# Row maxima of two attentions as pairs of 16-bit numbers, turned by 16-bit products, and their subtraction put first in each run on the row halves

## What is computed

```python
q = (layer_norm(x) @ wq)   # 20 heads of 64
k = (ctx @ wk); v = (ctx @ wv)   # ctx is layer_norm(x) itself in the self-attention
scores = einsum('bhnd,bhmd->bhnm', q, k) * 64 ** -0.5
attn = softmax(scores, axis=-1)
out = einsum('bhnm,bhmd->bhnd', attn, v)
x = out @ wo + bo + x
```

## Time and profile before

| | |
|---|---|
| Time, median of 3 runs | 1470.73 us |
| The profiled execution: its time, its span | 1475.56 us, 1473.8 us |
| TensorE matmuls (PE) busy | 1360.7 us, 92% |
| TensorE weight loads (PEld) busy | 1169.2 us, 79% |
| VectorE (DVE) busy | 1025.4 us, 70% |
| ScalarE (ACT), GpSimd (POOL) busy | 748.2 us, 751.0 us (51% each) |
| Mean granted clock of TensorE | 0.929 of full speed |
| Self-attention: maxima from, last weighing | 353.9 us, about 737 us |
| Cross-attention: maxima from, last weighing | 766.5 us, about 1372 us |

### The profile page before, as it was taken

One profiled execution on the slowest core, in us unless ns is written; L12 is line 12 of the kernel. 1 busy time (PEld: TensorE's weight loads), 2 busy tenths in 40 slices (PEclk: granted clock), 3 DMA queues, 4 the chain that ended last, 5 costly groups with the idle time before them and its releaser, 6 DMA issues. The chain is left out here.

```text
span 1473.8 us, 38650 instructions
## 1 busy us (share of the span) xinstructions
PE 1360.7 (92%) x16460; PEld 1169.2 (79%) x16460; DVE 1025.4 (70%) x1902; ACT 748.2 (51%) x1356; POOL 751.0 (51%) x510
## 2 busy tenths in 40 slices
PE   4989899885999999999979999999999999999597
PEld 3777777764888898889857888888888888888587
DVE  4577777746777867786657777777777767665485
ACT  2356565552555554555425545454555555554264
POOL 2266777565434443444514545454555555455364
PEclk9588888967999999999978999999999999999699
DMA  5001110002000000000010000000010000000000
GB/s 131 12 10 46 47 32 2 2 2 65 2 2 2 2 2 2 2 2 2 2 39 7 2 7 2 7 2 7 2 45 2 2 2 2 2 2 2 12 15 23
DMA packets 31955, 20.33 MB, mean 14 GB/s; under 512 B 21414, under 2 KB 30314, under 8 KB 31786
## 3 DMA queue, kind: packets, MB, share of 16 engines
q1 hardware_dynamic: 31786, 17.86, 4.7%
HBM read 16.54 MB, written 1.31 MB: 12 GB/s over the span
## 5 line engine op out<-in xcount | busy, mean ns | idle before, releaser
L507 POOL TENSOR_TENSOR cross_probs_l<-cross_probs 128x1024 f16<-128x1024 f32 x160 | 303.6, 1897 | 276.5 <-ACT cross_probs L578 276.2
L578 ACT ACTIVATE cross_probs<-cross_score 128x1024 f32<-128x1024 f32 x160 | 163.9, 1024 | 249.9 <-PE cross_score L820 249.9
L507 POOL TENSOR_TENSOR self_probs_l<-self_probs 128x1024 f16<-128x1024 f32 x80 | 151.5, 1894 | 204.0 <-ACT self_probs L578 203.6
L675 DVE TENSOR_REDUCE cross_maxima<-cross_max 128x2 f32<-128x1024 f32 x160 | 194.6, 1216 | 7.4 <-PE cross_max L796 7.2
L1591 POOL TENSOR_TENSOR ad_probs_l<-ad_probs 128x1024 f16<-128x1024 f32 x64 | 120.8, 1893 | 97.7 <-ACT ad_probs L1668 97.0
L578 ACT ACTIVATE self_probs<-self_score 128x1024 f32<-128x1024 f32 x80 | 82.1, 1027 | 156.8 <-PE self_score L820 156.8
L840 PEld LDWEIGHTS cross_pv<-cross_v_h,cross_probs 128*128 128x128 bf16 x1280 | 116.6, 98 | 33.2 <-issue 28.2
L840 PE MATMUL cross_pv<-cross_v_h,cross_probs 128*128 128x65 bf16 x1280 | 135.3, 196 | 2.6 <-POOL cross_probs_l L507 2.6
L661 DVE TENSOR_TENSOR cross_qk_l<-cross_shared,cross_qk_h 128x256 fp32r<-128x256 f32 (+1 forms) x160 | 87.9, 556 | 69.0 <-ACT cross_qk_h L563 68.8
L841 PE MATMUL cross_pv<-cross_v_l,cross_probs 128*128 128x64 f16 x1280 | 133.9, 194 | 0.0
L842 PE MATMUL cross_pv<-cross_v_h,cross_probs_l 128*128 128x65 bf16 x1280 | 133.5, 193 | 0.0
(11 more groups left out here) (420 smaller groups left out, 4735.5 us busy)
## 6 DMA issues: line engine op xcount, KB each, us to landing
ad_ctx_rows<-in_ctx SPq DMA_DIRECT2D x8, 192.0 KB, 2.8
cross_ctx_rows<-in_ctx SPq DMA_DIRECT2D x8, 192.0 KB, 2.5
sw_raw<-in_L_xattn_wq SPq DMA_DIRECT2D x2, 640.0 KB, 6.2
sw_raw<-in_L_xattn_wk SPq DMA_DIRECT2D x2, 640.0 KB, 4.3
sw_raw<-in_L_xattn_wv SPq DMA_DIRECT2D x2, 640.0 KB, 3.8
cw_raw<-in_L_xattn_wq SPq DMA_DIRECT2D x2, 640.0 KB, 4.1
lr_raw<-in_L_xattn_w_ff SPq DMA_DIRECT2D x2, 640.0 KB
out<-x_rows SPq DMA_DIRECT2D x8, 160.0 KB, 1.9
```

The lines of the kernel that those rows point to most:

```text
L507: nc.gpsimd.tensor_tensor(probs_l[:, n % PR, :, :].rearrange("p j k -> p (j k)"), whole, whole.bitcast(BF16)[:, 1::2], ALU.subtract).then_ ...
L578: nc.scalar.activation(probs[:, n % PR, :, :].rearrange("p j k -> p (j k)"), score_bank[:, :], ACT.Exp, scale=SCALE).then_inc(exped, 1)
L675: nc.vector.reduce_max(out, scores, AX.X).then_inc(max_read, 1)
```

## The change

Four things change in `attention`, in both attentions:

1. `reduce_max` writes float32 maxima to a small tile `top`. GpSimd writes them as a bfloat16 number and the bfloat16 remainder to columns 0 and 1 of `maxima`, which is now a bfloat16 tile (`split_maxima`, two instructions on 128x4 elements for each pair). It stands in GpSimd's list ahead of the low part of the last round of the slot.
2. "mt" waits for that (`max_split`) instead of `max_read`, and turns the two blocks by bfloat16 products with a bfloat16 identity, instead of float32 transposes.
3. `turned` and `minus` are bfloat16. The product with minus ones adds both parts.
4. The product with minus ones leaves `score` for a function `less_max`, and is issued ahead of `find_max`.

```diff
--- before.py
+++ after.py
@@ -392,7 +392,8 @@
         half_neg = sb("half_neg", [P, QT], F32)
         eps = sb("eps", [P, QT], F32)
         stats_seen = sb("stats_seen", [P, QT], F32)
-        minus = sb("minus", [P, P], F32R)
+        minus = sb("minus", [P, P], BF16)
+        ident_b = sb("ident_b", [P, P], BF16)
 
         xn = sb("xn", [P, QT, 2, P], F32)
         stats = sb("stats", [P, QT, 6], F32)
@@ -410,8 +411,9 @@
         qk_l = sb("qk_l", [P, KEPT, SEQ + KD], F32R)
         v_h = [sb(f"v_h{i}", [P, KT, HEADS, DV], BF16) for i in range(2)]
         v_l = [sb(f"v_l{i}", [P, KT, HEADS, DH], F16) for i in range(2)]
-        maxima = sb("maxima", [P, 2, QT, 2, DH], F32)
-        turned = sb("turned", [P, 2, SEQ], F32R)
+        top = sb("top", [P, 2, QT, 2], F32)
+        maxima = sb("maxima", [P, 2, QT, 2, DH], BF16)
+        turned = sb("turned", [P, 2, SEQ], BF16)
         PR = 2 * ROUNDS
         probs = sb("probs", [P, PR, 2, 512], F32)
         probs_l = sb("probs_l", [P, PR, 2, 512], F16)
@@ -446,6 +448,8 @@
         qk_hi = sem("qk_hi")
         max_filled = sem("max_filled")
         max_read = sem("max_read")
+        max_hi = sem("max_hi")
+        max_split = sem("max_split")
         scored = sem("scored")
         exped = sem("exped")
         probs_split = sem("probs_split")
@@ -491,17 +495,27 @@
                 pool.wait_ge(wo_hi, 1)
                 nc.gpsimd.tensor_tensor(wo_hl[:, :, 1, :], background.wo, wo_hl[:, :, 0, :], ALU.subtract).then_inc(wo_split, 1)
 
+            def split_maxima(batch, p):
+
+                b, _ = batch
+                pool.wait_ge(max_read, b * RB + (p + 1) * ROUNDS)
+                nc.gpsimd.tensor_copy(maxima[:, p % 2, :, :, 0], top[:, p % 2, :, :]).then_inc(max_hi, 1)
+                pool.wait_ge(max_hi, b * PAIRS + p + 1)
+                nc.gpsimd.tensor_tensor(maxima[:, p % 2, :, :, 1], top[:, p % 2, :, :], maxima[:, p % 2, :, :, 0],
+                                        ALU.subtract).then_inc(max_split, 1)
+
             def slot(kind, s, cur, prev, nxt):
                 if s == 2 and nxt is not None:
                     inverse_root(nxt[0])
                 if s == 4 and prev is not None:
                     rows = x[:, bass.ds(prev[0] * QT, QT), :]
                     nc.gpsimd.tensor_tensor(rows, rows, bo_row[:, None, :].to_broadcast([P, QT, HID]), ALU.add).then_inc(x_bo_ready, 1)
-                if (work := before(s, SCORE, cur, prev)) is not None:
-                    (b, _), p = work
-                    for r in range(ROUNDS):
+                for r in range(ROUNDS):
+                    if r == ROUNDS - 1 and (work := before(s, MAX, cur, prev)) is not None:
+                        split_maxima(*work)
+                    if (work := before(s, SCORE, cur, prev)) is not None:
+                        (b, _), p = work
                         n = p * ROUNDS + r
-
                         pool.wait_ge(exped, b * RB + n + 1)
                         whole = probs[:, n % PR, :, :].rearrange("p j k -> p (j k)")
                         nc.gpsimd.tensor_tensor(probs_l[:, n % PR, :, :].rearrange("p j k -> p (j k)"), whole,
@@ -517,7 +531,8 @@
             pool.wait_ge(filler, 1)
             inverse_root(0)
 
-            nc.gpsimd.memset(minus[:, :].bitcast(F32), -1.0)
+            nc.gpsimd.memset(minus[:, :], -1.0)
+            nc.gpsimd.tensor_copy(ident_b[:, :], ident[:, :])
             nc.gpsimd.memset(maxima[:, :, :, :, :], 0.0)
             for i in range(2):
                 ins = nc.gpsimd.memset(v_h[i][:, :, :, DH:DV], 1.0)
@@ -668,9 +683,9 @@
                         (b, _), p = work
                         dve.wait_ge(max_filled, b * RB + p * ROUNDS + r + 1)
                         if cross:
-                            out, scores = maxima[:, p % 2, r, :, 0], max_bank[:, :].rearrange("p (j k) -> p j k", j=2)
+                            out, scores = top[:, p % 2, r, :], max_bank[:, :].rearrange("p (j k) -> p j k", j=2)
                         else:
-                            out = maxima[:, p % 2, :, :, 0].rearrange("p t j -> p j t")
+                            out = top[:, p % 2, :, :].rearrange("p t j -> p j t")
                             scores = max_bank[:, :].rearrange("p (j t k) -> p j t k", j=2, t=QT)
                         nc.vector.reduce_max(out, scores, AX.X).then_inc(max_read, 1)
                     if s == 3 and r == 0 and nxt is not None:
@@ -802,17 +817,19 @@
                                                   qk_h[half, at, t * P:(t + 1) * P], qk_h[half, at, SEQ:SEQ + KD], start=True, stop=True)
                 mm.then_inc(max_filled, 1)
 
-            def score(r, work):
+            def less_max(r, work):
 
                 (b, parity), p = work
-                at = kept(parity, p)
-                n = p * ROUNDS + r
                 if r == 0:
                     pe.wait_ge(shifted, b * PAIRS + p + 1)
-                after(pe, exped, b * RB + n)
+                after(pe, exped, b * RB + p * ROUNDS + r)
                 for j, half in enumerate(HALF):
                     nc.tensor.matmul(score_bank[:, j * 512:(j + 1) * 512].rearrange("p (c q) -> p c q", c=2), minus[half, :],
                                      turned[half, p % 2, None, :].to_broadcast([DH, 2, SEQ]), start=True, stop=False)
+
+            def score(r, work):
+                (b, parity), p = work
+                at = kept(parity, p)
                 for c in range(2):
                     keys = slice(SEQ + (2 * r + c) * P, SEQ + (2 * r + c + 1) * P)
                     for m, (ks, qs) in enumerate(((qk_h, qk_h), (qk_h, qk_l), (qk_l, qk_h))):
@@ -846,6 +863,8 @@
             def slot(kind, s, cur, prev, nxt):
                 period = cur[0] if cur is not None else NB
                 for r in range(ROUNDS):
+                    if (work := before(s, SCORE, cur, prev)) is not None:
+                        less_max(r, work)
                     if (work := before(s, MAX, cur, prev)) is not None:
                         find_max(kind, s, r, work, period)
                     if (work := before(s, SCORE, cur, prev)) is not None:
@@ -856,10 +875,10 @@
                         if key[0] == "mt":
                             (b, _), p = before(s, MT, cur, prev)
                             bank_ = claim(kind, period, key)
-                            pe.wait_ge(max_read, b * RB + (p + 1) * ROUNDS)
+                            pe.wait_ge(max_split, b * PAIRS + p + 1)
                             for t in range(QT):
-                                mm = nc.tensor.transpose(bank_[:, t * P:(t + 1) * P],
-                                                         maxima[:, p % 2, t, :, :].rearrange("p j c -> p (j c)"), ident[:, :])
+                                mm = nc.tensor.matmul(bank_[:, t * P:(t + 1) * P], maxima[:, p % 2, t, :, :].rearrange("p j c -> p (j c)"),
+                                                      ident_b[:, :], start=True, stop=True)
                             mm.then_inc(filled, 1)
                         elif key[0] == "weigh":
                             weigh(kind, s, key[1], before(s, WEIGH, cur, prev))
```

10 lines of the change are left out of this document (5 added, 5 removed).

## The result

The changed kernel takes 1451.74 us (median of 4 runs, 1449.74 to 1455.42), the kernel before beside it 1469.87 us (4 runs, 1464.77 to 1471.73): ratio 0.987, interval 0.985 to 0.989. It is 18 us faster. I had forecast 42 us, a time of 1429. The time lies inside the range that I had stated, 1418 to 1456, but by luck: the range reached that high only for two rivals, neither of which holds as I had put it, and the sum's own range ended at 1437.

The account below looks back on a forecast made before the run. TensorE's instruction pace was taken to bound both attentions. 26.4 + 19.7 - 2 - 1.4 - 1 = 41.7 us saved, median 1470.7 to 1429 us; range 1418 to 1456, the sum's own 1420 to 1437.

Parts of the forecast that it names:

- opening of the runs: Start of each run on TensorE: 16-bit minus ones first save 0.11 us in 240 runs, 26.4 us.
- turned maxima: Turning on TensorE: 16-bit products save 0.11 us before F32R (108) and 0.15 otherwise (52), 19.7 us.
- GpSimd (tight pairs, once): Delayed low parts cost 2 us over 16 tight pairs; late split maxima in the first self-attention batch cost 1.4 us once.
- last slots: Waits moved to the front of the run cost 1 us, in the last slots, where little lies between runs.
- as slow as the 4-byte one: Bound on the opening: if a 16-bit load on a row half is that slow (187 ns), it saves nothing.
- the first rival: The opening gains nothing, by a slow half-row load or a pause between types: 16 us saved, 1455 us; chance 0.13.
- 0.12, 0.23, 0.23: Expected TensorE distances in us: last `weigh` product to minus ones, these to maxima, maxima to scores.
- The slower pace: Turned maxima at the skill's 81 ns per 128-column product: pair 0.16 instead of 0.11 us, term 8 us smaller.
- comes off the time nearly in full: Both attentions: TensorE sets the pace, so savings between two starts in its timeline shorten the time almost fully.
- one slot per batch where it leads: Against the no-change rival (1468 us, chance 0.05): VectorE, at 74%, leads in only one slot per batch.
- 0.4 us are left: Worst cross-attention slot: the delayed low part ends at about 1012.3, `weigh` needs it at 1012.78; two pairs in ten so tight.
- GpSimd's order costs more: Rival: a pair of small instructions takes 1.4 us, stalling 16 tight pairs, 11 us more, 1440 us; chance 0.09.

Follow-up runs that it names:

- one16_maxima_first: `one16` with the minus ones put back behind the maxima, leaving only the turned maxima by 16-bit products: 1461.00 us, ratio 0.994 to the kernel before.
- one16: The changed kernel without its GpSimd part; reduce_max writes each maximum once as a 16-bit number, no split: 1434.48 us.
- 1: Experiment 1, the run `one16`: the changed kernel without its GpSimd part, each maximum kept as one 16-bit number: 1434.48 us.
- 2: The changed kernel, but in the self-attention alone GpSimd issues the low part first and splits the maxima behind it: 1441.58 us.
- 3: The kernel before plus only GpSimd's wait for the maxima ahead of the last low part, no new work: 1478.94 us.
- 10: Experiment 10, the run `one16_norm_later`: `one16` with VectorE taking the second round's maxima before splitting the layer norm, cross-attention only: 1447.83 us.
- one16_norm_later: `one16`, but in the cross-attention VectorE takes the maxima of a slot's second round before splitting the layer norm: 1447.83 us.
- maxima_first: The changed kernel with the minus ones back behind the maxima, so the maxima open the run again: 1471.04 us.

## Why the prediction was wrong

By the stages, which leave out the adapter, the sum reads so:

```
                               forecast   by the stages
opening of the runs              26.4        22.6     one16_maxima_first to one16
turned maxima                    19.7        11.8     before to one16_maxima_first
GpSimd (tight pairs, once)       -3.4       -11.8     one16 to after
last slots                       -1.0         -       inside the other rows
sum                              41.7        22.6     before to after
```

The medians say 18 for the sum and 17 for GpSimd's part; the adapter of the profiled execution of `one16` was 6 us shorter than that of the changed kernel, at a granted clock of 0.87 against 0.82, which may account for that. The middle batches with the clock at 1.00 give, for self- and cross-attention together, 2.70 us per batch for the opening, 1.41 for the turned maxima and -1.61 for GpSimd's part; times 8 that is 21.6, 11.3 and -12.9, near the stages. Of the last slots, TensorE's waits for the exponential and for `turned` at the minus ones grew from 0.7 to 1.8 us in all, 1.1 where I had put 1.

**The opening, 240 x 0.11: right as a distance, 22.6 of 26.4 us as time.** The distance became 0.10 us shorter in the rows shown and 0.11 in the median over all runs; the 16-bit load on a half takes 93 ns against 187, so the bound "as slow as the 4-byte one" is out, and with it the first rival. I had written what the trace would show as 0.12, 0.23, 0.23. It shows 0.13, 0.04, 0.42: the sum is right and the split is not. The record of the F32R maxima starts 0.04 us behind the minus ones, but the 0.46 us from the minus ones to the scores are within 0.02 of two streams of 512 columns at the 0.22 of the prediction, so hardly any of their load is exposed. The Trainium skill (TensorE: Matmul & The Clock Gate, Weight-path perf modes) left open whether 64 rows get the fast load; the 93 ns beside 98 for full rows say that a half loads at the pace of full rows. Whether either is that fast load no run here shows.

**The turned maxima, 108 x 0.11 + 52 x 0.15: right as distances** (0.40 to 0.30, and 0.27 to 0.12), **mis-sized as time**: 19.7 forecast, 11.8 measured. The slower pace that I had set against my price was not met either: 0.12 us for the pair with what follows, where the Trainium skill's 81 ns each would make 0.16 by the estimate in the prediction.

**The first step that failed** is therefore the sentence that what is saved between two starts in TensorE's timeline "comes off the time nearly in full". I read VectorE's share as 74% over 40 and 74 us and saw "one slot per batch where it leads". Windows laid on single slots of the kernel before (the third engine is VectorE) show more. The last slot of one cross batch and the first two of the next, then the second and third slot of a self batch:

```profile
1064.47:1071.94 7.47, 7.47 (x102) 6.43 (x100) 6.36 (x14) 4.51 (x8) 4.69 (x4) 1.00 0.01 2
1071.94:1079.67 7.73, 7.73 (x101) 6.48 (x100) 7.70 (x13) 4.42 (x8) 4.62 (x3) 1.00 0.01 2
1079.67:1087.16 7.49, 6.89 (x99) 6.05 (x97) 6.44 (x13) 4.55 (x8) 3.81 (x2) 1.00 0.43 132
...
553.79:558.68 4.89, 4.22 (x58) 3.73 (x56) 4.81 (x11) 2.80 (x5) 2.01 (x2) 1.00 0.02 5
558.68:563.80 5.12, 5.01 (x63) 4.22 (x61) 5.01 (x11) 3.05 (x5) 1.89 (x1) 1.00 0.00 0
```

VectorE is busy for 7.70 of 7.73 us in the first slot of the cross batch, and for 4.81 of 4.89 and 5.01 of 5.12 in the two self slots. What is saved there turns into a wait: in `one16` TensorE waits for VectorE 1.01 and 0.42 us in these two self slots (0.67 and 0.11 before) and 0.26 in that cross slot (none before). In the second cross slot it waits 0.53 us for the maxima, nearly as before (0.60). By the slots of one batch in `one16` five in twenty give back little or nothing, those that keep 4.85, 5.22, 7.63, 7.27 and 7.03; had they gained 0.18 and 0.33 each like the others, a batch would have given 1.35 us there instead of 0.34, and the 7 batches that have a layer norm beside them 7 us more. A full VectorE alone does not tell: in the first slot of the self batch it is busy for 3.83 of 3.83 us, and that slot gave its 0.19. And in the third cross slot (7.11 to 7.03) it is busy for 5.42 us; why that one keeps its length is not shown. The other slots too gave 0.18 and 0.33 us where the two terms make 0.22 and 0.36; over some 7 slots in each of 8 batches and both attentions that is an estimated 3 to 4 us. Together these are some 10 to 11 of the 11.7 us by which the two terms fell short.

**The second step that failed** is the cost of GpSimd's part. I asked of the delayed low part only who waits for it (`weigh`, "0.4 us are left"), and that was right: those waits are 2.8 us, and the waits for the split maxima in the first self batch 2.0. (The small instructions number 320 and not 160, two for each pair.) I did not ask what the low part runs beside once it is late. The rival "GpSimd's order costs more" had the engine right and the victim wrong; it put 11 us on the pair's length, which is 0.42 us (0.20 + 0.22), as forecast. The loss came to that size in another way: VectorE's cast by 1.7 us in 6 of 8 self batches (1.80 in the slot), and in the cross batches 0.38 us in the second slot, where the cast takes 0.95 us instead of 0.57. Of the 11.8 us some 2.7 are the granted clock, 1.5 in the one slot of 8.43 us and 1.2 at the end of the cross-attention. (The 0.56 gained in the self-attention's second slot is of the same kind: of the four instructions that normalise the rows two met GpSimd before, with 2.03 and 0.91 us instead of 0.33 and 0.34, and with the later low part only one does, 1.92.)

The rule that says so was in my hands. The Trainium skill (SBUF — State Buffer, Who interferes with whom) has VectorE and GpSimd hold one port pair exclusively, whoever comes first, for copies and casts in SBUF as well as for two SBUF inputs. I had quoted it for two inputs alone and looked for its effect in the length of GpSimd's row, where it hardly shows, since VectorE's instructions are short. The row of 1.92 us that I took as evidence was none: what lies beside it in the earlier trace rows is `reduce_max`, which reads a PSUM bank. It shows in VectorE's, and the trace of the kernel before had it already, in the layer norm, beside a low part that runs from 551.17 to 553.06:

```profile
551.12 2.03 DVE L612 TENSOR_SCALAR self_xn<-x_rows,self_mean_var,self_rstd 128x128 f32<-128x128 f32 x1
553.07 0.91 DVE L610 TENSOR_SCALAR self_xn<-x_rows,self_mean_var,self_rstd 128x128 f32<-128x128 f32 x1
553.91 0.33 DVE L612 TENSOR_SCALAR self_xn<-x_rows,self_mean_var,self_rstd 128x128 f32<-128x128 f32 x1
```

One form, 0.33 and 2.03 us. (The 0.91 us lie beside GpSimd's addition to `x_rows`, 553.03 to 553.91.) That this is a lock on a port and not some other hold-up is the Trainium skill's account; the runs show which instructions lose, and that they end 0.1 to 0.3 us after GpSimd's.

**Shown and not shown.** That the late start of the low part makes the loss is shown from three sides (1 and 2 take it away, 3 makes it alone), the collision also from VectorE's side (10). The two self batches whose cast does not take 2.1 us beside a low part are no exceptions: in the first layer norm the cast takes 2.36 us beside GpSimd's splitting of the weights (2.67 in the kernel before), and in the second the low part starts at 365.46 and the fourth instruction, at 365.88, takes the blow (2.02 us). Why the granted clock falls behind some of the waits and not behind others is open. A version that moves the low part clear of both the layer norm and the turned maxima was not tried; `one16`, which needs no splitting, makes the question idle.

## What to carry to other kernels

A saving on the engine that sets the pace must be laid on single slots, and the second engine's busy share read slot by slot, with the waits at its end: a mean of 74% held slots at 98 to 100%. Where an edit delays an instruction, ask who waits for it and also what it will run beside. In these kernels a cast, a tensor with scalars or a two-input operation of VectorE with all operands in SBUF, put next to a GpSimd instruction of 1.9 us, cost up to 1.7 us more, and TensorE's wait for it another 1.5 us where the granted clock fell. And where 4-byte weights open a run behind a change to the row halves, a 16-bit product in front took away the 0.11 us of exposed load; in the middle of the run it did not, since the product that opens is still a 4-byte one.

## What the hardware showed that I had not expected

- VectorE's instructions with all operands in SBUF wait out GpSimd's 1.89 us: cast 0.43 to 2.12 us, subtraction with two SBUF inputs 0.42 to 2.02, tensor with scalars 0.33 to 2.03. In the same stretches those that read a PSUM bank keep their length: in the kernel before, `reduce_max` of 1.21 us at 555.90 lies beside the low part of 555.00.
- Behind waits of TensorE of 1.9 to 2.1 us the granted clock fell to 0.51 for a stretch in some batches and not in others: in 1 of 6 middle batches of the changed kernel's self-attention, 3 of 6 in `maxima_first`, 5 of 6 in the cross-attention of `one16_norm_later`. Each fall cost 1.5 us.
- Behind a 16-bit product on the row halves the record of the next F32R product starts 0.04 us later, though 512 columns are on their way; the time is found one row on (0.42 in front of the run, 0.30 to the second scores in the middle of it). Distances must be summed over several rows before two kernels are compared.
- A 16-bit product gains in front of the F32R ones and hardly anything between them: from the minus ones to the second scores it is 0.34 us there, and 0.36 in the kernel before.
